# Gathers issued in bursts of four, with a wait for the landing of each burst, in a two-layer graph network

## The reference

```python
edge_index = jnp.stack([src, dst])
h = jnp.maximum(_layernorm(x), 0.0)
x = x + gcn(h, edge_index, W, b)          # layer 0
h = jnp.maximum(_layernorm(x), 0.0)
x = x + attention(h, edge_index, ...)     # layer 1

# layer 0, with self loops added:
norm = dinv[src] * dinv[dst]
out  = relu(segment_sum((x @ W)[src] * norm[:, None], dst) + b)

# layer 1, 8 heads of 16:
q = src_rows @ Wq.T + bq ; k, v = tgt_rows @ Wk.T + bk, tgt_rows @ Wv.T + bv
e = exp(clip((q * k).sum(per head) / 4, -10, 10))
out = segment_sum(e / (segment_sum(e)[rows] + 1e-8) * v, rows) + node_embeds
out = layernorm(out) * gamma + beta
```

## Time and profile before

| | |
|---|---|
| time, three runs | 3014.48, 3023.04, 3029.83 us |
| median | 3023.04 us |
| span of the profiled execution | 2933.4 us |
| PE busy | 1928.0 us, 66% |
| DVE busy | 1877.1 us, 64% |
| POOL busy | 1551.6 us, 53% |
| ACT busy | 1134.3 us, 39% |
| gathers of layer 0 | 832, from 120.28 to 1425.45 us |
| gathers of layer 1 | 672, from 1557.77 to 2852.98 us |

### The profile page before, as it was taken

The page is one execution under the profiler, slowest core; times in us unless marked ns, Lnnn a source line. Parts: engine busy times, 40 slices in busy tenths (PEclk is TensorE's granted clock), DMA queues, the critical chain, the costliest instruction groups (busy, mean ns, idle before and its releaser), DMA issues. The chain is left out here.

```text
span 2933.4 us, 44454 instructions
## 1 busy us (share of the span) xinstructions
PE 1928.0 (66%) x11165; PEld 1544.6 (53%) x11166; DVE 1877.1 (64%) x5088; ACT 1134.3 (39%) x3135; POOL 1551.6 (53%) x1594
## 2 busy tenths in 40 slices
PE   5324347666767756677685777767777777777772
PEld 4323334444444434445465676666666676666662
DVE  9858876555655745555584666666666666666666
ACT  8524356555655645656562121111121122111123
POOL 0266656656656556566244555555455455555454
PEclk7766668778878878788897889898888888889886
DMA  3211111111111111111034222222222222223222
GB/s 105 62 43 43 46 38 44 43 41 43 40 38 43 40 39 40 37 45 43 22 121 113 80 82 75 75 75 79 75 82 80 77 82 77 81 77 88 78 76 47
DMA packets 114287, 184.52 MB, mean 63 GB/s; under 512 B 29293, under 2 KB 75373, under 8 KB 114133
## 3 DMA queue, kind: packets, MB, share of 16 engines
q0 software_dynamic: 61136, 147.00, 18.5%
q1 hardware_dynamic: 22501, 22.03, 2.4%
q10 hardware_dynamic: 30624, 15.21, 2.1%
HBM read 165.51 MB, written 18.62 MB: 63 GB/s over the span
## 5 line engine op out<-in xcount | busy, mean ns | idle before, releaser
L296 POOL DMA_INDIRECT rows<-y_tab,idx x832 | 793.6, 954 | 566.9 <-issue 303.3
L1314 POOL DMA_INDIRECT x<-kv_tab,kv_idx x672 | 685.8, 1021 | 628.9 <-DVE msg L1366 416.2
L1534 PE MATMUL ps_kv<-kv_s,hot_low 128*128 x1362 | 384.0, 420 | 173.6 <-DVE hot_low L1338 77.2
L773 ACT ACTIVATE sort_v<-sort_t,staged,minus 128x128 f16<-128x128 f16 x914 | 360.7, 480 | 314.5 <-remote 272.4
L865 PE MATMUL ps_sort<-sort_hi,sort_v 128*128 128x496 f16 x1662 | 408.0, 397 | 107.6 <-issue 105.7
L1459 ACT ACTIVATE by_tile<-ps_hT 128x512 f32<-128x512 f32 x226 | 134.9, 597 | 872.9 <-remote 420.1
L612 DVE TENSOR_SCALAR sort_v<-iota_h,staged 128x128 f16<-128x128 f16 x748 | 244.1, 326 | 354.2 <-remote 304.2
L823 PE MATMUL ps_sum<-rows,hot 128*128 128x128 f32 x1664 | 284.3, 326 | 237.3 <-issue 121.6
L823 PEld LDWEIGHTS ps_sum<-rows,hot 128*128 128x128 f32 x1664 | 263.8, 238 | 258.2 <-issue 162.0
L1534 PEld LDWEIGHTS ps_kv<-kv_s,hot_low 128*128 128x128 f32 x1362 | 266.6, 209 | 223.9 <-issue 193.2
L1348 DVE TENSOR_TENSOR by_tile<-ps_q,x 128x512 f32<-128x512 f32 x224 | 154.7, 691 | 339.7 <-remote 183.0
(11 more groups left out here) (289 smaller groups left out, 2198.2 us busy)
## 6 DMA issues: line engine op xcount, KB each, us to landing
weights<-tile_tab ACTq DMA_DIRECT2D x58, 256.0 KB
rows<-y_tab,idx POOLq DMA_INDIRECT x832
x<-kv_tab,kv_idx POOLq DMA_INDIRECT x672
kv_tab<-kv_s SPq DMA_DIRECT2D x12, 512.0 KB
x<-x_in SPq DMA_DIRECT2D x1, 3328.0 KB, 13.4
out<-x SPq DMA_DIRECT2D x12, 256.0 KB
out<-h POOLq DMA_DIRECT2D x12, 256.0 KB, 7.3
by_slot<-tile_tab SPq DMA_DIRECT2D x1, 1452.0 KB, 13.1
```

The source lines that it names most:

```text
L296: pool.indirect_dma_start(out=rows[:, k * SPAN + n, :], out_offset=None, in_=y_tab, in_offset=bass.IndirectOffsetOnAxis(ap=idx[:, k, n:n + ...
L773: last = nc.scalar.activation(to[:, k % 2, m, :], sort_t[:, k % 2, m, :], ACT.Relu, bias=staged[:, v, c:c + 1], scale=minus[:, v, c:c + 1])
L1314: pool.indirect_dma_start(out=rows[:, u, k, :], out_offset=None, in_=kv_tab, in_offset=bass.IndirectOffsetOnAxis(ap=idx[:, u, k:k + 1], ax ...
L1534: last = nc.tensor.matmul(ps_kv[:, k % 2, :], hot_low[:, w, k * P:(k + 1) * P], kv_s[:, ds(low + w, 1), :], start=w == 0, stop=w == WINDOW ...
```

## The change

POOL issues its gathers four at a time and waits for the landing of each four before it issues the next. In layer 0 a group of eight becomes two bursts of four (`BURST = SPAN // 2`), with a wait after the first burst and one after the second. In layer 1 a quad has four gathers, and the wait stands after them. Beside this, waits of DVE and PE whose threshold is computed in a register now go through a helper that takes the maximum of the threshold and zero first and adds a `nop`; and the number of the last pass is clamped in the same way.

```diff
+BURST = SPAN // 2
...
+    def wait_positive(engine, semaphore, value):
+
+        with engine.register() as bounded:
+            engine.reg_alu(bounded, value, 0, ALU.max)
+            engine.wait_ge(semaphore, bounded)
+            engine.nop(nofuse=True)
...
                         for n in range(SPAN):
+                            if n == BURST:
+                                pool.wait_ge(rows_in[k], i * (16 * SPAN) + 16 * BURST)
+                                pool.nop(nofuse=True)
                             pool.indirect_dma_start(
                                 out=rows[:, k * SPAN + n, :], out_offset=None, in_=y_tab,
                                 in_offset=bass.IndirectOffsetOnAxis(ap=idx[:, k, n:n + 1], axis=0),
                             ).then_inc(rows_in[k], 16)
+                        pool.wait_ge(rows_in[k], (i + 1) * (16 * SPAN))
...
-                    v.wait_ge(more_rel_set, more + b + 1)
+                    wait_positive(v, more_rel_set, more + b + 1)
...
-                    v.wait_ge(more_done, more + b + 1)
+                    wait_positive(v, more_done, more + b + 1)
...
-                                    v.wait_ge(more_acc, more + b + 1)
+                                    wait_positive(v, more_acc, more + b + 1)
...
-                                pe.wait_ge(more_ready, more + b + 2)
+                                wait_positive(pe, more_ready, more + b + 2)
...
                                 out=rows[:, u, k, :], out_offset=None, in_=kv_tab,
                                 in_offset=bass.IndirectOffsetOnAxis(ap=idx[:, u, k:k + 1], axis=0),
                             ).then_inc(rows_in[u], 16)
+                        pool.wait_ge(rows_in[u], (i + 1) * (16 * QUAD))
...
-                end = loads(mybir.EngineType.DVE, passes_tab[0:1, 1:2], PASSES - 1)[0]
+                last_pass = v.alloc_register()
+                v.reg_alu(last_pass, loads(mybir.EngineType.DVE, passes_tab[0:1, 1:2], PASSES - 1)[0], 0, ALU.max)
+                end = v.snap(last_pass, min_val=0, max_val=PASSES - 1)
```

More of the change, by code:

```diff
@@ L508, in edges @@
                                 with v.Fori(lo + 1, hi) as b:
-                                    v.wait_ge(more_acc, more + b + 1)
+                                    wait_positive(v, more_acc, more + b + 1)
                                     more_hots(i, k, b, more)
                                     add_more(b, more)
-                            v.wait_ge(more_acc, more + hi + 1)
+                            wait_positive(v, more_acc, more + hi + 1)
                             more_hots(i, k, hi, more)
@@ L667, in _ @@
                     add_more(highs[0], mores[0])
-                    v.wait_ge(more_acc, mores[0] + highs[0] + 2)
+                    wait_positive(v, more_acc, mores[0] + highs[0] + 2)
                     v.nop(nofuse=True)
```

## The result

The changed kernel takes 3124.19 us (median of 4 runs, 3123.38 to 3125.77), the kernel before beside it 3018.76 us (4 runs, 2998.31 to 3029.83). The ratio is 1.036, 95% interval [1.032, 1.040]: slower by 105 us. I had forecast slower, but 3283 us with a range from 3140 to 3450, so the time lies outside. Of the four runs of the kernel before three are those from ahead of the prediction; the fourth, 2998.31 us, came with the result.

What follows compares the result with a forecast made beforehand. The PE, DVE and ACT chain bounds the kernel before; after the change POOL does. Layer 0 +228 and layer 1 +32 us on the 2933.4 span give 3193, plus 89.6 around it 3283 us; range 3140 to 3450.

Steps and rivals of the forecast that it cites:

- The 89.6 us around the span: Whole kernel: time outside the profiled span, added to the forecast span of 3193 us to give 3283.
- The pause: POOL, last issue of a burst to next issue: landing plus POOL's start, 2.8 us in layer 0, 3.0 in layer 1.
- So POOL is 0.68 slower than PE to react: Restart after a wait: POOL starts 0.82 us after DVE's read, PE 0.14 after ACT; 0.68 added to the landing.
- PE's 2.08 and 2.17: Start of layer 0: two times from gather issue end to PE's start, taken as a landing of 2.1 us.
- The formula of the Trainium skill: Gather landing: about 2.0 us plus bytes over 436 thousand per us, so 2.15 for 64 KB, 2.30 for 128 KB.
- the clamps cost nothing: Clamped waits of DVE and PE: taken as nothing while POOL is the bound, at most 58 us.
- Layer 1's part of the growth: Layer 1's gathers: POOL barely the bound, 168 bursts of 7.98 us, +32 us.
- Rival 2: Both layers: landings slower under load, 3.4 us, pause 4.08, 3731 us, halfway near 3500; chance with its half 0.15.
- Rival 3: Both layers: nothing changes, since POOL's spare time swallows the pause; chance 0.03.
- Rival 1: PE's slow stretches, ACT's and DVE's unnamed waits: pauses between gathers relieve them; faster, 2892 us, pause below 2.1; chance 0.10.
- 1.56 and 2.73 us to spare per burst: POOL before the change, layers 0 and 1: time left per burst of four, usual 0.30 gap included.
- The rule on fetching code behind a taken branch: PE's slow stretches: a branch outside buffered pages stalls the engine; layer 1 would give back up to 5.8 us a pass.

Runs made afterwards that it cites:

- e7: The changed kernel with each POOL wait asking for older gathers, and fewer waits (190): 2318.85 us, ratio 0.999 to the kernel before beside it.
- e3: The changed kernel with all three of POOL's waits out, only the clamps of DVE and PE kept: 2317.31 us, ratio 0.998 to the kernel before beside it.
- e1: The changed kernel with layer 1's wait taken out, layer 0's waits and the clamps kept: 2762.07 us, ratio 1.190 to the kernel before beside it.
- e2: The changed kernel with layer 0's waits taken out, layer 1's wait and the clamps kept: 2684.95 us, ratio 1.157 to the kernel before beside it.
- e6: The changed kernel without the wait in the middle of layer 0's groups, so bursts of eight there: 2911.97 us, ratio 1.255 to the kernel before beside it.

## Why the prediction was wrong

The profiled execution after takes 3123.4 us, the forecast was 3283, and the miss of 160 us has two terms, 88 and 72 us.

**The 89.6 us around the span: 88 of them.** I added the difference between the span of the profiled execution (2933.4) and the median of other runs as if it were launch time. The profiled execution after has a span of 3121.7 and a time of 3123.38: 1.7 us lie around it, and 1.6 to 1.8 in every run of the experiments. By that the profiled execution of the kernel before took some 2935 us, 63 to 95 less than its four timed runs. That is inferred, since it has no time on record. Scatter of this kind was itself a sign: the three runs that I had spread over 15 us, the changed kernel's four over 2.4. With 1.7 in its place the same sum gives 3195 us. The step that failed is "with the 89.6 us around it": if POOL's own period is the bound, as I had it, what else slows the kernel before doesn't come on top. It is also why the growth is 105 us against the timed runs and 188 against the profiled execution.

**The pause: 72 us.** The step that failed is "So POOL is 0.68 slower than PE to react", and with it the landing in it. POOL's pause is 2.31 us (420.8 us over the 182 pauses named by the DMA) where I had 2.8. The trace also holds the times at which the semaphores were raised, and they split it. In the changed kernel the landing is there 1.57 us after the end of the issue in layer 0 (mean; 1.45 to 1.71 but for one pause, 2.08), and POOL's next issue starts 0.74 us after it in the middle of a group and 0.76 at its head. So POOL's slow reaction did carry over: the 0.82 of the earlier trace rows is seen again in e7, at all 55 bursts that waited for DVE, and for a landing it is only a little less. What was wrong is what stood beside it. I took PE's 2.08 and 2.17 as a landing with the 0.14 of an ACT semaphore in it, which makes the landing 1.96. At the same two places in e3 the landing comes 1.60 and 1.61 us after the end of the issue, and PE starts 0.51 and 0.54 after that: PE's program has a branch and further waits between its wait for the rows and the first product. So POOL reacts 0.2 us later than PE does there, and not 0.68. In layer 0 that made 7.52 us per burst instead of 7.15: 1561 forecast for the window, 1489 measured.

In layer 1 two errors cancelled. The pause was 2.68, not 3.0, but an issue took 1.078 us on average, not the 1.021 of the earlier trace rows, and the gaps 0.32. Each burst took 7.95 us against my 7.98, so 1335 against 1338. That more bytes land later was right in sign and size: the landing comes 1.77 us after the end of the issue in layer 1 against 1.57, 0.2 more for 64 KB more, where the queue's rate had given 0.24. The pauses named by the DMA are 2.58 there (289.4 us over 112) against 2.31. The formula of the Trainium skill (DMA: Bandwidth & Descriptors, "Anatomy of one DMA — SWDGE (gpsimd) path") gives an estimate of 0.15 for this difference and 2.15 and 2.30 in all. Counted from the start of the issue, some 0.95 us earlier, the landings here come after about 2.5 and 2.7 us, so the formula is low by 0.4 and the difference near. That its totals are close to the pauses of 2.31 and 2.58 is chance, since these leave out the issue and have POOL's restart in them.

**What held.** POOL became the bound in both layers, the waiting moved to the DMA, the clamps cost nothing where POOL is the bound (e3), and the cost is the number of pauses times their length (e1, e2, e6). Layer 1's part of the growth was +32 forecast and +30.4 measured; that this is so near is luck, since two errors cancel in it. The direction was right, for the reason that was given.

**The rivals.** Rival 2 (slower landings under load) fell: the longest of the 374 pauses in the changed kernel is 3.24 us, their means are 2.36 and 2.68, and where nothing waits for the landing (e3) it takes as long, 1.58 and 1.79 us (medians). Rival 3 fell. Rival 1 did not decide, since by its own terms it needed a pause under 2.1 us and the pauses are 2.36 and 2.68. But what it had seen was the important thing: the stretches are gone in the changed kernel. That the pauses took them away isn't shown.

**What bounds the kernel before: right for that trace, and not the rule.** I wrote that the chain of PE, DVE and ACT sets the pace and that POOL has 1.56 and 2.73 us to spare per burst. In the profiled execution that is so. But the spare time is made of the slow stretches: without them the same order of work (e3) has a span of 2318 us, 616 less, of which 1305.2 - 1049.6 = 256 lie in layer 0's window and 1295.2 - 966.7 = 328 in layer 1's, and POOL has next to nothing to spare. The change costs 105 us in the recorded result and 802 and 810 us on the two chips where both kernels ran, and all follow from one sentence: the changed kernel takes the 3124 us that POOL's pauses set, whatever it is compared with.

**What stays open** is what the slow stretches are. This is DVE in the kernel before, single instructions with 1 to 4 us between them, and below it the same work in e3, pairs without a gap:

```profile
156.70 0.65 DVE L553 COPY_PREDICATED cols<-dhi,ps_sort 128x440 f32<-128x440 uint16 x1 [1.05 <-issue]
159.50 0.60 DVE L553 COPY_PREDICATED cols<-dhi,ps_sort 128x400 f32<-128x400 uint16 x1 [2.15 <-issue]
164.41 1.14 DVE L547 TENSOR_TENSOR_SCAN ps_sort<-dlo,first,ps_iota 128x440 f32<-128x440 f16 x1 [4.31 <-issue]
166.51 1.05 DVE L547 TENSOR_TENSOR_SCAN ps_sort<-dlo,first,ps_iota 128x400 f32<-128x400 f16 x1 [0.96 <-issue]
```

```profile
151.08 2.06 DVE L555 TENSOR_TENSOR_SCAN ps_sort<-dhi,first,ps_iota 128x440 f32<-128x440 f16 x2
153.06 1.12 DVE L561 COPY_PREDICATED cols<-dhi,ps_sort 128x440 f32<-128x440 uint16 x2
```

Nearly all of the idle time named "remote" is waiting for PE: the semaphores waited for are those that PE's products raise, for 1462 of 1470 us. They rose late, 1.5 to 30 us after the end that the profile gives to the last product before it (median 6.0 over 275 waits); in e3 it is 0.01 us at all 460 waits that PE ended. The first group's sum shows it: by the profile PE ends it at 132.44 + 3.75 = 136.19, but its semaphore rises at 147.56, and DVE adds it at 147.79; in e3 the semaphore rises at 136.17 and DVE adds the sum at 141.77. Before and e3:

```profile
147.79 0.29 DVE L479 TENSOR_TENSOR acc<-acc,ps_sum 128x128 f32 x1 [3.09 <-remote]
...
141.77 0.27 DVE L487 TENSOR_TENSOR acc<-acc,ps_sum 128x128 f32 x1
```

The stretches aren't matrix work alone, since DVE has them too, and PE's lower clock isn't their cause: the changed kernel is granted as little (0.75 and 0.86 against 0.76 and 0.88) and has none. The rule on fetching code behind a taken branch, which I had weighed (the Trainium skill, Runtime: NRT & Kernel Launch, "Instruction fetch mechanics"), isn't borne out: the queues that fetch instructions moved as little with the stretches as without them.

```profile
q8 instruction: 9, 0.15, 0.0%
q14 instruction: 17, 0.14, 0.0%
```

These are the rows of before; after and every experiment have 9 and 18 packets. None of them starts between 435 and 960 us in the kernel before, and the stretch of the earlier trace rows lies at 618 to 632. The gathers' own queue wasn't slow either: 18.5% of 2933.4 us is 543 us, and 23.3% of 2317.8 in e3 is 540. Two readings remain. A condition of that chip or of that session disturbed the kernel before, and had passed when the changed one ran or does not reach it. That it had passed is the less likely, as far as the fourth run of the kernel before, 2998.31 us, was taken beside the changed one; where and when isn't noted. Or under that condition the unbroken stream of gathers brings the stretches on and the pauses take them away, which is rival 1. On the three chips of the experiments the unbroken stream brought on nothing. No experiment ran while the stretches were there, so it wasn't settled.

## What to carry to other kernels

An indirect gather is issued by POOL, so count its issue and the gap behind it before saying that POOL has time: here 1.26 us each, which is the whole of layer 0. A wait for the landing of the gather just issued then costs a pause each time, 2.3 to 2.7 us with the restart in it. A wait for gathers that were issued four gathers ago in layer 0, three in layer 1, costs nothing (e7); a kernel that must hold a strict bound would need it at the first group of each body too, which wasn't run. A reaction time read from one pair of engines is to be used for the same place in the program, not only for the same engine: PE started 0.14 us after ACT in one place and 0.5 after a landing in another. And where the profiled span lies far below the timed runs, or engines pause with no releaser that the profile can name, the baseline is suspect: a sum made on its spare time holds for that baseline alone.

## What the runs showed of the hardware

- The idle time from the end of a gather's issue on POOL to POOL's next issue, when it waits for that landing: 2.31 us for 64 KB and 2.58 for 128 KB (means of 182 and 112), with at most 2.5 and 2.7. Of this the landing takes 1.57 and 1.77 us and POOL's restart 0.74 to 0.76 and 0.81.
- Other engines start sooner after a landing: PE 0.41 to 0.68 us (46 waits of `ps_sum` in the changed kernel, with a branch and other waits in between), DVE 0.02 us (110 waits).
- POOL's pauses whose end the profile calls "issue" are longer than those named by the DMA, 2.75 against 2.31 in layer 0 (25 of 207) and 2.87 against 2.58 in layer 1 (55 of 167). They stand at the turns of the loop, and at no other place: there POOL's restart takes 1.16 and 1.11 us, 0.40 and 0.30 more than at the head of the other bursts.
- POOL's mean issue in layer 1 is 1.078 us after, 1.086 in e3 and 1.021 in the disturbed profile before, while in layer 0 it is 0.95 to 0.96 in all of them.
- The same program takes 3019 us in one session and 2321 on three chips in others, with 34 runs there inside 7 us.
